# A transformer block on one core: the score products of a head pair moved from 122 shared rows to two 64-row halves of TensorE's array, with four slots and new instruction orders

## The chip, the cores and the metric

The kernel runs on one core of a Trainium2 chip. The metric is the device time of one execution in microseconds. Before the change the median of 3 runs is 1230.65 us (1229.91 to 1230.84).

## What is computed

The reference is one transformer block with adaptive layer norms for 32 sequences of 256 tokens and 288 channels, 16 heads of 18 channels, all in float32:

```python
B, L, C, H, D, FF = 32, 256, 288, 16, 18, 1152
ada = silu(c) @ W_ada + b_ada            # six vectors of 288 per sequence
shift_msa, scale_msa, gate_msa, shift_mlp, scale_mlp, gate_mlp = split(ada, 6)
h = layernorm(x) * (1 + scale_msa) + shift_msa
q, k, v = split_heads(h @ W_qkv + b_qkv)
attn = softmax((q * D ** -0.5) @ k.T)    # per head, 256 x 256
x = x + gate_msa * ((attn @ v) @ W_proj + b_proj)
h = layernorm(x) * (1 + scale_mlp) + shift_mlp
x = x + gate_mlp * (gelu(h @ W_fc1 + b_fc1) @ W_fc2 + b_fc2)
```

## The kernel before

The work goes sequence by sequence ("batch" b), and every engine runs a list of steps written out by hand: a head (`PE_HEAD` and so on), a period that is repeated for one batch after another (`PE_ORDER`), and a tail. An entry such as ("s", 1, 4) in a period for batch k is step `s` of batch k + 1 with number 4. `run` plays the lists. Between engines there are only semaphores, so a step that waits holds up all that stands behind it on its engine. Several batches are in flight: the scores of batch k, the projections of k + 2, the MLP of k - 2 and k - 3.

The matrix products take fp32r operands, split in a rounded part and a rest, so each projection is seven products (`products`): `xt` and `lt` turn the normalised tokens, `qk` and `v` project (bank `x_bank`), `proj`, `fc1`, `fc2` follow (banks `a_bank`, `b_bank`).

Attention works on pairs of heads: 8 pairs j per batch, in two halves of `HP` = 4. The q and k rows of a half are written to DRAM from `qst` (`qkw`) and read back (`qkr`, 13 DMAs per half) into slots of `ql` and `kl`. Three slots are used in turn (`half_use`). The rows of the contraction are a head's 54 rows (hi, lo and cross parts of 18 channels), at partitions 0 to 53 for head 0 and 68 to 121 for head 1, with four rows between at 64 to 67 (`MXR`). These four carry the row maxima: `kl` holds -1 in row 64 + j for pair j, `ql` the maximum of each query, so that the product gives scores minus maximum. `ql` has a block of its own for either head (index i), with zeros at the rows of the other head, and both heads share one `kl` block. One product contracts over all 122 rows.

- `s(b, j)` (L808) makes the scores of both heads, 2 products of 256 columns for each, into `score_bank[i]`. VectorE takes their maxima (`head_max`, L1138), transposes them (`mt`), and ScalarE copies them into the four rows of `ql` (`mb`, L946), 8 copies per half.
- `st(b, j)` (L822) makes the transposed scores less the maxima, 2 products of 512 columns (both heads at once), into `st_bank` of two PSUM banks; ScalarE takes `exp` into `e` (L953).
- `pv(b, half)` (L834) multiplies with v for the half: 16 fp32 products of 256 columns, each recorded as two, for four pairs in turn in four column tiles of 32.

In a slot that is used again, the four maxima rows must be zero before `s` runs; the 13th read of `qkr` (m == 12) does this by a DMA from a DRAM tensor `zeros` (L617). On SyncE's queue the reads of a half wait for the last `st` of the half that had the slot before.

```python
for i in range(2):
    wait(pe, s_max[i], PAIRS * b + j)
    for t in range(NT):
        last = nc.tensor.matmul(score_bank[i][:, t * L:(t + 1) * L],
                                ql[0:KM, slot, i, j % HP, t * P:(t + 1) * P], kl[0:KM, slot, j % HP, :],
                                start=True, stop=True)
    last.then_inc(s_full[i], 1)
```

Of the kernel before, what the change touches and what calls it, by code (L numbers as in the profile page):

```python
# [14 lines left out]
D = C // H  # L15
FF = 4 * C
EPS = 1e-6
P = 128
# [8 lines left out]
MXR = 64  # L27
HB = MXR + PAIRS // 2
KM = HB + KS
# [9 lines left out]
SLOTS = 3  # L39
# [4 lines left out]
READS = 13  # L44
# [32 lines left out]
    ("max", 0, 4), ("ln1_apply", 2, 0), ("max", 0, 5), ("om", -2, 1), ("qk", 1, 1), ("max", 0, 6), ("ol", -2, 1),  # L77
    ("max", 0, 7), ("fc1", -3, 4), ("rcp", -1, 0), ("mt", 0, 0), ("proj", -2, 0), ("proj", -2, 1), ("qk", 1, 2),
# [1262 lines left out]
```

## Time and profile before

| | |
|---|---|
| median of 3 runs | 1230.65 us |
| profiled execution | 1228.32 us |
| its span, first to last instruction | 1226.5 us |
| TensorE products busy | 1181.1 us, 96% |
| TensorE weight loads busy | 1064.3 us, 87% |
| VectorE busy | 901.8 us, 74% |
| ScalarE busy | 866.1 us, 71% |
| GpSimd busy | 540.3 us, 44% |
| mean granted TensorE clock | 0.993 |

How to read it. "PE" is TensorE's products, "PEld" its weight loads, DVE is VectorE, ACT ScalarE, POOL GpSimd, SP SyncE. A product's recorded duration includes its way through the array, so products overlap in the records; what one costs the queue is the distance from its start to the next start. Weight loads run ahead of products. A group row ends with the engine's idle time just before that group and what ended it.

### The profile page before, as it was taken

Reading aid. Unit: us, or ns where it says so; the run is one execution under the profiler, and the core shown is the slowest. Engines: PE = TensorE matmul, PEld = TensorE weight load, DVE = VectorE, ACT = ScalarE, POOL = GpSimd, SP = SyncE. Lnnn points to the kernel's source line nnn. Section 1 sums busy time; section 2 is a strip of 40 time slices with the busy share of each in tenths; the row PEclk is TensorE's granted clock in tenths of the full one; section 3 lists DMA queues with packets and bytes.
Section 4 is the critical chain, followed back from the end, with each engine's and each line's share of the span. In section 5 each row is a group of like instructions: output and inputs, shape, how many; then the busy total and the mean of one; then the engine's idle time right before and its main releaser. Section 6 shows DMA issues by size and latency. Waiting matters only on the chain.

```text
span 1226.5 us, 27564 instructions
## 1 busy us (share of the span) xinstructions
PE 1181.1 (96%) x9863; PEld 1064.3 (87%) x9863; DVE 901.8 (74%) x1928; ACT 866.1 (71%) x1485; POOL 540.3 (44%) x557
## 2 busy tenths in 40 slices
PE   6888999999999999999999999999999999999977
PEld 5666999999998999999999999999999999997777
DVE  5687777877777787778777777777777787775553
ACT  5387777777777777777777777777777777778721
POOL 3012544444454444445454444444444445443364
PEclk9799999999999999999999999999999999999999
DMA  8554555554555554445555444555554555444220
GB/s 265 171 169 138 167 167 164 164 154 144 163 160 159 168 166 145 157 157 162 167 166 164 147 159 150 166 165 167 161 153 148 158 166 159 162 149 140 87 68 20
DMA packets 134330, 188.91 MB, mean 154 GB/s; under 512 B 24544, under 2 KB 102422, under 8 KB 133947
## 3 DMA queue, kind: packets, MB, share of 16 engines
q1 hardware_dynamic: 134033, 186.71, 48.3%
q8 instruction: 80, 1.31, 0.5%
q10 hardware_dynamic: 162, 0.44, 0.1%
q14 instruction: 55, 0.45, 0.1%
HBM read 121.92 MB, written 64.63 MB: 152 GB/s over the span
## 4 chain that ended last, share of the span: by engine, by line
PE 84%; SPq 5%; DMA 4%; DVE 3%; ACT 2%; issue 1%; POOL 0%; ACTq 0%; POOLq 0%; DVEq 0%
PE a_bank L867 10%; PE x_bank L785 10%; PE score_bank L808 9%; PE turn_bank L834 9%; PE st_bank L822 9%; PE b_bank L867 8%; PE b_bank L881 6%; PE b_bank L882 5%; PE b_bank L883 5%; PE a_bank L848 4%; PE x_bank L793 4%; SPq L623 2%; DMA qk_rows<-qst 1%; DMA ql<-zeros 1%; PE x_bank L759 1%
## 5 line engine op out<-in xcount | busy, mean ns | idle before, releaser
L1138 DVE TENSOR_REDUCE mx<-score_bank 128x2 f32<-128x512 f32 x512 | 342.0, 687 | 95.8 <-PE score_bank L808 93.7
L953 ACT ACTIVATE e<-st_bank 128x1024 f32<-128x1024 f32 x256 | 262.4, 1025 | 125.8 <-PE st_bank L822 123.5
L1287 POOL TENSOR_TENSOR gl<-gl_raw,gh 128x512 fp32r<-128x512 f32 (+1 forms) x160 | 194.3, 1221 | 226.4 <-DVE gh L1203 226.4
L946 ACT CAST ql<-mxt 4x256 fp32r<-4x256 f32 x512 | 206.2, 403 | 7.4 <-DVE mxt L1147 0.6
L808 PEld LDWEIGHTS score_bank<-kl,ql 122*128 122x128 f32 x1024 | 146.9, 190 | 42.0 <-issue 24.4
L808 PE MATMUL score_bank<-kl,ql 122*128 122x256 f32 x1024 | 174.6, 293 | 5.6 <-DMA ql<-zeros 3.3
L881 PE MATMUL b_bank<-w,gh 128*128 128x288 f32 x576 | 174.5, 303 | 2.2 <-DVE tmp L1209 1.9
L822 PE MATMUL st_bank<-ql,kl 122*128 122x512 f32 x512 | 165.7, 405 | 7.7 <-ACT e L953 6.9
L882 PE MATMUL b_bank<-w,gh 128*128 128x288 f32 x576 | 170.5, 296 | 0.0
L883 PE MATMUL b_bank<-w,gl 128*128 128x288 f32 x576 | 170.3, 296 | 0.0
L834 PE MATMUL turn_bank<-e,ve 128*32 128x256 f32 x2048 | 123.8, 382 | 0.3 <-ACT e L953 0.3
L881 PEld LDWEIGHTS b_bank<-w,gh 128*128 128x128 f32 x576 | 108.8, 189 | 4.1 <-DVE tmp L1209 2.6
L867 PE MATMUL a_bank<-xh,w 128*128 128x256 f32 x640 | 105.4, 287 | 6.4 <-DVE xr L1117 4.4
L882 PEld LDWEIGHTS b_bank<-w,gh 128*128 128x128 f32 x576 | 108.9, 189 | 0.1
L883 PEld LDWEIGHTS b_bank<-w,gl 128*128 128x128 f32 x576 | 108.5, 188 | 0.0
L785 PE MATMUL x_bank<-xh,wq 128*128 128x256 f32 x632 | 103.1, 286 | 1.5 <-ACT xl_raw L920 0.8
L1203 DVE CAST gh<-gl_raw 128x512 fp32r<-128x512 f32 (+1 forms) x160 | 85.9, 551 | 18.6 <-ACT gl_raw L991 16.8
L834 PEld LDWEIGHTS turn_bank<-e,ve 128*32 128x32 f32 x2048 | 60.1, 110 | 43.0 <-issue 4.9
L1299 POOL TENSOR_TENSOR x<-tmp,x 128x288 f32<-128x288 f32 x64 | 51.8, 810 | 99.2 <-DVE tmp L1209 99.0
L867 PEld LDWEIGHTS a_bank<-xh,w 128*128 128x128 f32 x640 | 87.9, 191 | 8.7 <-issue 8.7
L822 PEld LDWEIGHTS st_bank<-ql,kl 122*128 122x128 f32 x512 | 79.8, 190 | 15.2 <-ACT e L953 10.4
L981 ACT ACTIVATE xl_raw<-a_bank,mod 128x256 f32<-128x256 f32 (+1 forms) x96 | 50.6, 561 | 59.8 <-PE a_bank L759 54.2
(152 smaller groups left out, 2473.1 us busy)
## 6 DMA issues: line engine op xcount, KB each, us to landing
qk_rows<-qst SPq DMA_DIRECT2D x128, 256.0 KB, 5.3
ql<-qk_rows SPq DMA_DIRECT2D x384, 72.0 KB
kl<-qk_rows SPq DMA_DIRECT2D x378, 72.0 KB
o_rows<-on SPq DMA_DIRECT2D x128, 128.0 KB
gate<-gates SPq DMA_DIRECT2D x32, 432.0 KB, 4.4
xin<-in_x SPq DMA_DIRECT2D x32, 288.0 KB, 5.9
x<-in_x SPq DMA_DIRECT2D x32, 288.0 KB, 3.0
out<-x SPq DMA_DIRECT2D x32, 288.0 KB, 4.5
```

Source lines behind the costliest of these rows:

```text
L785: last = nc.tensor.matmul(bank[:, k * L:(k + 1) * L], wa[:, c * P:(c + 1) * P], xa, start=(i == 0), stop=(i == len(pr) - 1))
L808: last = nc.tensor.matmul(score_bank[i][:, t * L:(t + 1) * L], ql[0:KM, slot, i, j % HP, t * P:(t + 1) * P], kl[0:KM, slot, j % HP, :], st ...
L822: last = nc.tensor.matmul(st_bank[:, u, :, :], kl[0:KM, slot, j % HP, u * P:(u + 1) * P], ql[0:KM, slot, :, j % HP, :], start=True, stop=True)
L834: last = nc.tensor.matmul(turn_bank[VB * c:VB * (c + 1), q * L:(q + 1) * L], ve[:, b % 2, u, 8 * half + 2 * c + q, :], e[:, c, u, q, :], s ...
L867: last = nc.tensor.matmul(bank[:, (f % 2) * L:(f % 2 + 1) * L], wa[:, f * P:(f + 1) * P], xa, start=(i == 0), stop=(i == len(pr) - 1))
L881: nc.tensor.matmul(b_bank[:, 0:C], gh[:, cols], w2[:, 0, f, :], start=(f == 0), stop=False)
L882: nc.tensor.matmul(b_bank[:, 0:C], gh[:, cols], w2[:, 1, f, :], start=False, stop=False)
L883: last = nc.tensor.matmul(b_bank[:, 0:C], gl[:, cols], w2[:, 0, f, :], start=False, stop=(f == NF - 1))
L946: last = nc.scalar.copy(rows[:, :, :, t, a, :], src)
L953: nc.scalar.activation(e[:, j % 4, :, :, :].rearrange("p u i l -> p (u i l)"), st_bank[:, :, :, :].rearrange("p u i l -> p (u i l)"), ACT. ...
L1138: nc.vector.tensor_reduce(mx[:, j // HP, i, :, col:col + 1], score_bank[i][:, :].rearrange("p (t l) -> p t l", t=NT), AX.X, ALU.max).then_ ...
L1287: nc.gpsimd.tensor_tensor(gl[:, cols], g[:, cols], gh[:, cols].bitcast(F32), ALU.subtract).then_inc(g_lo, 1)
```

## The change

The two heads of a pair get separate halves of the partitions. Head i has its rows from 64 i on: four rows for the maxima, then its 54 rows, 58 in all (`KM`). `ql` and `kl` lose the index for the head and the zero blocks, and each product contracts over the 58 rows of one head. In the built program these products have an array tile of 64 rows by 128 columns, at row 0 or 64, where they had the whole 128 by 128. `s` has 4 products of 256 columns as before, now issued t by t with the two heads in turn, after both waits. `st` has 4 products of 256 columns (two for each head, heads in turn) instead of 2 of 512, each head in its own bank of `st_bank`; `e` is laid out to match. The instruction that makes `exp` has the same size.

There are four slots instead of three. The four maxima rows are cleared by a GpSimd fill over rows 0 to 67 of the slot (`clear`, step "clr"), which waits for the last `st` of the half that had the slot, and `qkr` waits for the clear; the 13th read and the DRAM tensor `zeros` go, and there are 12 reads per half. The -1 rows of `kl` come from the identity matrix (`chosen`), by four ScalarE copies at the start, in place of fills, four DMAs and two ScalarE clears of `ql`.

The lists of all engines are new. Counted in the built programs, TensorE's queue changes its array tile 164 times before and 705 times after; in the repeated period it is 4 and 21 times. The period has 16 score steps (`s` or `st`); in the new list they stand in nine places, seven of two steps and two of one.

```diff
-MXR = 64
-HB = MXR + PAIRS // 2
-KM = HB + KS
+TILE = 64
+KM = PAIRS // 2 + KS
-SLOTS = 3
+SLOTS = 4
-READS = 13
+READS = 12
 PE_ORDER = [
-    ("fc2", -3, 2), ("pv", -1, 1), ("s", 0, 4), ("fc2", -3, 3), ("st", 0, 0), ("v", 1, 0), ("fc2", -3, 4),
...
+    ("fc2", -3, 0), ("proj", -2, 0), ("st", 0, 1), ("s", 0, 6), ("xt", 2, 0), ("proj", -2, 1), ("st", 0, 2),
...
-        ql = sb("ql", [P, SLOTS, 2, HP, L], F32R)
+        ql = sb("ql", [P, SLOTS, HP, L], F32R)
-        e = sb("e", [P, 4, NT, 2, L])
+        e = sb("e", [P, 4, 2, NT, L])
...
-            row = (0, HB)[i] + D * r
-            to = ql[row:row + D, slot, i, :, :] if w == 0 else kl[row:row + D, slot, :, :]
+            row = TILE * i + HP + D * r
+            to = (ql if w == 0 else kl)[row:row + D, slot, :, :]
...
-                    if use == 0:
-                        sp.wait_ge(consts, ROWS_SET)
-                        wait(sp, rows_cleared, slot)
-                    else:
-                        before = b * HALVES + half - SLOTS
-                        sp.wait_ge(st_full, PAIRS * (before // HALVES) + HP * (before % HALVES + 1))
-                if m == 12:
...
-                        sp.dma_start(ql[MXR:MXR + HP, slot, :, :, :].rearrange("p i j l -> p (i j l)").bitcast(F32),
-                                     zero_dram).then_inc(qk_rows[slot], 16)
-                    return
+                    if b == 0 and half == 0:
+                        sp.wait_ge(kl_chosen, SLOTS)
+                    sp.wait_ge(ql_cleared, HALVES * b + half + 1)
...
                 for i in range(2):
                     wait(pe, s_max[i], PAIRS * b + j)
-                    for t in range(NT):
+                for t in range(NT):
+                    for i in range(2):
+                        rows = slice(TILE * i, TILE * i + KM)
                         last = nc.tensor.matmul(score_bank[i][:, t * L:(t + 1) * L],
-                                                ql[0:KM, slot, i, j % HP, t * P:(t + 1) * P], kl[0:KM, slot, j % HP, :],
+                                                ql[rows, slot, j % HP, t * P:(t + 1) * P], kl[rows, slot, j % HP, :],
                                                 start=True, stop=True)
-                    last.then_inc(s_full[i], 1)
+                        if t == NT - 1:
+                            last.then_inc(s_full[i], 1)
...
                 for u in range(NT):
-                    last = nc.tensor.matmul(st_bank[:, u, :, :], kl[0:KM, slot, j % HP, u * P:(u + 1) * P],
-                                            ql[0:KM, slot, :, j % HP, :], start=True, stop=True)
+                    for i in range(2):
+                        rows = slice(TILE * i, TILE * i + KM)
+                        last = nc.tensor.matmul(st_bank[:, i, u, :], kl[rows, slot, j % HP, u * P:(u + 1) * P],
+                                                ql[rows, slot, j % HP, :], start=True, stop=True)
...
+            for u in range(SLOTS):
+                nc.gpsimd.memset(ql[0:TILE + HP, u, :, :].bitcast(F32), 0.0).then_inc(ql_cleared, 1)
+
+            def clear(b, half):
+                slot, use = half_use(b, half)
+                if use:
+                    before = b * HALVES + half - SLOTS
+                    pool.wait_ge(st_full, PAIRS * (before // HALVES) + HP * (before % HALVES + 1))
+                    nc.gpsimd.memset(ql[0:TILE + HP, slot, :, :].bitcast(F32), 0.0).then_inc(ql_cleared, 1)
```

How this moves TensorE's queue, first at the second `pv` of a period. Line numbers are those of either program; names are bank <- operands; `score_bank` is step `s`, `st_bank` step `st`, `turn_bank` step `pv`, `a_bank` and `b_bank` with `xh`, `xl`, `xr` are `fc1`, `x_bank` with `wq` is `qk`, `b_bank` with `gh`, `gl` is `fc2`. Before:

```order
L822 MATMUL st_bank<-ql,kl 128x512 x2
L808 MATMUL score_bank<-kl,ql 128x256 x4
L762 MATMUL x_bank<-ident,xn 96x128 x2
L867 MATMUL b_bank<-xh,w 128x256 x4
...
L834 MATMUL turn_bank<-e,ve 32x256 x16
L808 MATMUL score_bank<-kl,ql 128x256 x4
L867 MATMUL a_bank<-xh,w 128x256 x4
```

and after the change:

```order
L793 MATMUL score_bank<-kl,ql 128x256 x4
L822 MATMUL turn_bank<-e,ve 32x256 x16
L855 MATMUL a_bank<-xh,w 128x256 x4
L855 MATMUL a_bank<-xl,w 128x256 x2
L855 MATMUL a_bank<-xr,w 128x256
```

The score step stands in front of `pv` here and behind it before; the `st` step has 4 products of 256 columns in the new program. The next place is inside the period, between the MLP's products. Before:

```order
L785 MATMUL x_bank<-xr,wq 128x256
L808 MATMUL score_bank<-kl,ql 128x256 x4
L867 MATMUL b_bank<-xh,w 128x256 x4
L867 MATMUL b_bank<-xl,w 128x256 x2
L867 MATMUL b_bank<-xr,w 128x256
...
L867 MATMUL a_bank<-xr,w 128x256
L822 MATMUL st_bank<-ql,kl 128x512 x2
L808 MATMUL score_bank<-kl,ql 128x256 x4
```

and after:

```order
L871 MATMUL b_bank<-w,gl 128x288
L793 MATMUL score_bank<-kl,ql 128x256 x4
L810 MATMUL st_bank<-ql,kl 128x256 x4
L855 MATMUL a_bank<-xh,w 128x256 x4
...
L855 MATMUL a_bank<-xr,w 128x256
L793 MATMUL score_bank<-kl,ql 128x256 x4
L810 MATMUL st_bank<-ql,kl 128x256 x4
L768 MATMUL x_bank<-xh,wq 128x256 x4
```

A single score step and a pair of them stood here before; now the steps come in pairs with whole-array products between. Last, GpSimd's queue behind a `clr` in the new program:

```order
L1279 TENSOR_TENSOR x<-tmp,x 128x288
L1232 MEMSET ql 68x1024
L1285 TENSOR_TENSOR gl<-gl_raw,gh 128x256
L1279 TENSOR_TENSOR x<-tmp,x 128x288
L1262 TENSOR_TENSOR xl<-xl_raw,xh 128x512
```

The fill is new; what stood there before was the same subtraction (`fc1`) and residual additions (`proj`) without it.

## Rows read from the trace of the kernel before

**Rows 1.** The page's first part, and its chain of waits by engine

```profile
PE 1181.1 (96%) x9863; PEld 1064.3 (87%) x9863; DVE 901.8 (74%) x1928; ACT 866.1 (71%) x1485; POOL 540.3 (44%) x557
PE 84%; SPq 5%; DMA 4%; DVE 3%; ACT 2%; issue 1%; POOL 0%; ACTq 0%; POOLq 0%; DVEq 0%
```

**Rows 2.** Stretches: from:to and length, busy us (instructions) of each engine, clock, DMA

```profile
170.00:1050.00 880.00, 878.88 (x7504) 804.60 (x7506) 679.55 (x1458) 657.57 (x1132) 410.37 (x419) 1.00 0.50 159
600.50:636.13 35.63, 35.63 (x305) 32.66 (x304) 27.45 (x60) 26.69 (x46) 16.83 (x17) 1.00 0.54 168
0.00:100.00 100.00, 78.22 (x547) 60.42 (x547) 67.63 (x152) 58.11 (x97) 17.82 (x28) 0.93 0.65 196
```

**Rows 3.** Groups of instructions by line, 170 to 1050 us

```profile
L1138 DVE TENSOR_REDUCE mx<-score_bank 128x2 f32<-128x512 f32 x394 | 264.5, 687 | 70.4 <-PE score_bank L808 68.6
L953 ACT ACTIVATE e<-st_bank 128x1024 f32<-128x1024 f32 x199 | 204.0, 1025 | 104.3 <-PE st_bank L822 102.9
L946 ACT CAST ql<-mxt 4x256 fp32r<-4x256 f32 x392 | 157.9, 403 | 5.2
L1287 POOL TENSOR_TENSOR gl<-gl_raw,gh 128x512 fp32r<-128x512 f32 (+1 forms) x121 | 145.7, 1212 | 172.4 <-DVE gh L1203 172.4
L808 PE MATMUL score_bank<-kl,ql 122*128 122x256 f32 x784 | 131.8, 291 | 0.0
L822 PE MATMUL st_bank<-ql,kl 122*128 122x512 f32 x396 | 126.9, 402 | 1.1 <-ACT e L953 1.1
```

**Rows 4.** Timeline of TensorE's products: start us, us until the last ends

```profile
617.99 0.63 PE L822 MATMUL st_bank<-ql,kl 122*128 122x512 f32 x2
618.46 0.64 PE L808 MATMUL score_bank<-kl,ql 122*128 122x256 f32 x4
618.93 0.38 PE L762 MATMUL x_bank<-ident,xn 128*96 128x128 f32 x2
```

**Rows 5.** The same view around a `pv` step

```profile
604.74 0.29 PE L883 MATMUL b_bank<-w,gl 128*128 128x288 f32 x1
604.97 1.93 PE L834 MATMUL turn_bank<-e,ve 128*32 128x256 f32 x32
606.83 0.74 PE L808 MATMUL score_bank<-kl,ql 122*128 122x256 f32 x4
607.41 0.30 PE L881 MATMUL b_bank<-w,gh 128*128 128x288 f32 x1
```

**Rows 6.** The same view, products in flight at 606.49

```profile
606.28 0.40 PE L834 MATMUL turn_bank<-e,ve 128*32 128x256 f32 x4
```

**Rows 7.** Timeline of weight loads, those begun by 605.05 us

```profile
604.96 0.16 PEld L834 LDWEIGHTS turn_bank<-e,ve 128*32 128x32 f32 x8 [0.16 <-issue]
```

**Rows 8.** Timeline of weight loads around the same `pv` step

```profile
604.61 0.19 PEld L883 LDWEIGHTS b_bank<-w,gl 128*128 128x128 f32 x1
...
606.83 0.54 PEld L808 LDWEIGHTS score_bank<-kl,ql 122*128 122x128 f32 x4 [0.41 <-issue]
607.30 0.19 PEld L881 LDWEIGHTS b_bank<-w,gh 128*128 128x128 f32 x1
```

**Rows 9.** Timeline of weight loads of the modulation products

```profile
50.71 0.53 PEld L732 LDWEIGHTS st_bank<-rcb,e 128*128 128x128 f32 x4
51.28 0.30 PEld L732 LDWEIGHTS st_bank<-rcb,gh_raw 33*128 33x128 f32 x2
51.62 0.52 PEld L732 LDWEIGHTS st_bank<-rcb,e 128*128 128x128 f32 x4
```

**Rows 10.** Who waited for the DMAs that read `zeros`

```profile
  PEld score_bank L808: 5.4, 6
  PE score_bank L808: 3.3, 5
```

**Rows 11.** GpSimd's fills at the start, groups by line

```profile
L1233 POOL MEMSET kl<- 128x3072 f32 x1 | 2.7, 2657 | 3.8 <-DVE rcb L1033 3.8
L1234 POOL MEMSET ql<- 128x2048 f32 x1 | 1.8, 1822 | 0.0
```

More of the change, by code:

```diff
@@ new lines @@
+    ("max", 0, 11), ("ln1_stats", 3, 0), ("proj", -2, 0), ("fc1", -3, 4), ("max", 0, 12), ("max", 0, 13),
+    ("proj", -2, 1), ("rcp", -1, 1), ("max", 0, 14), ("max", 0, 15), ("xt", 2, 0), ("mt", 0, 1),
+    ("ln2_stats", -2, 0), ("xt", 2, 1), ("sum2", -3, 0), ("ln2_apply", -2, 0), ("ln2_apply", -2, 1), ("max", 1, 0),
+    ("max", 1, 1), ("qk", 2, 0), ("lt", -2, 0), ("max", 1, 2), ("max", 1, 3), ("lt", -2, 1), ("ln1_apply", 3, 0),
+    ("max", 1, 4), ("max", 1, 5), ("qk", 2, 1), ("sum2", -3, 1), ("max", 1, 6), ("max", 1, 7),
@@ L101 @@
+    ("or", -1, 0), ("qkr", 1, 12), ("qkr", 1, 13),
 ]
@@ L133 @@
+    ("v", 0, 0), ("qkr", 0, 0), ("v", 0, 1), ("qkr", 0, 1), ("qkr", 0, 2), ("qkr", 0, 3), ("qkr", 0, 4),
+    ("round", 0, 2), ("qkr", 0, 5), ("xt", 1, 0), ("xt", 1, 1), ("qk", 1, 0), ("round", 0, 3), ("round", 0, 4),
[9 rows of a table added]
 ]
 DVE_HEAD = [
[3 rows of a table removed]
-    ("max", 0, 2), ("max", 0, 3), ("ln1_apply", 2, 0), ("ln1_apply", 2, 1), ("max", 0, 4), ("max", 0, 5),
-    ("qk", 1, 1), ("max", 0, 6), ("max", 0, 7), ("mt", 0, 0), ("qk", 1, 2), ("max", 0, 8), ("max", 0, 9),
-    ("gates", 0, 0), ("mod", 0, 0), ("split", 0, 2), ("max", 0, 10), ("max", 0, 11), ("split", 0, 3), ("max", 0, 12),
@@ new lines @@
+    ("qkw", 3, 1), ("rr", 0, 1), ("qkw", 3, 2), ("rr", 0, 2), ("rr", 0, 3), ("or", 0, 4), ("rr", 0, 4), ("rr", 0, 5),
+    ("or", 0, 5), ("ow", 1, 0), ("qkr", 3, 0), ("qkw", 3, 3), ("sr", 1, 0), ("ow", 1, 1), ("qkr", 3, 1),
+    ("qkr", 3, 2), ("qkr", 3, 3), ("qkr", 3, 4), ("qkr", 3, 5), ("qkw", 3, 4), ("qkr", 3, 6), ("qkr", 3, 7),
+    ("qkr", 3, 8), ("qkr", 3, 9), ("qkr", 3, 10), ("sr", 1, 1), ("qkr", 3, 11), ("ow", 1, 2), ("ow", 1, 3),
+    ("sw", 1, 0), ("qkr", 3, 12), ("or", 1, 0), ("qkr", 3, 13),
@@ L224 @@
[L224 to L227 removed]
[10 rows of a table removed]
+    ("om", -4, 0), ("mt", -2, 0), ("max", -2, 8), ("fc1", -5, 0), ("fc1", -5, 1), ("qk", -1, 2), ("max", -2, 9),
@@ L270 @@
+    ("qkr", -1, 18), ("qkr", -1, 19), ("qkr", -1, 20), ("or", -3, 3), ("ow", -2, 0), ("rr", -3, 5), ("qkr", -1, 21),
[7 rows of a table added]
+    ("store", -2, 0), ("store", -1, 0),
 ]
@@ L698, in _ @@
                 load_weights(i)
-            sp.wait_ge(consts, ROWS_SET)
-            for jj in range(HP):
-                row = slice(MXR + jj, MXR + jj + 1)
-                sp.dma_start(kl[row, :, jj, :].bitcast(F32),
-                             tmp2[row, 0, 0:L].unsqueeze(1).broadcast_to([1, SLOTS, L])).then_inc(kl_rows, 16)
-            sp.dma_start(zero_dram, ql[MXR:MXR + HP, 0, :, :, :].rearrange("p i j l -> p (i j l)").bitcast(F32)
-                         ).then_inc(zeros_stored, 16)
             run(SYNC_HEAD, SYNC_ORDER, SYNC_TAIL, {"ln1_stats": ln1_stats, "res": res, "qkw": qkw, "qkr": qkr, "ow": ow,
@@ L903, in _ @@
             act.wait_ge(iota_step, 2)
-            for slot in range(1, SLOTS):
-                nc.scalar.activation(ql[:, slot, :, :, :].rearrange("p i j l -> p (i j l)"),
-                                     ident[:, 0:1].broadcast_to([P, 2 * HP * L]), ACT.Copy, scale=0.0
-                                     ).then_inc(rows_cleared, 1)
+            act.wait_ge(choice, 1)
+            for slot in range(SLOTS):
+                nc.scalar.activation(kl[0:TILE + HP, slot, :, :],
+                                     chosen[0:TILE + HP, :].unsqueeze(2).broadcast_to([TILE + HP, HP, L]), ACT.Copy,
+                                     scale=-1.0).then_inc(kl_chosen, 1)
             for i in range(N_FIRST):
@@ L941, in mb @@
                 act.wait_ge(mx_turned, HALVES * b + half + 1)
-                rows = ql[MXR:MXR + HP, slot, :, :, :].rearrange("p i j (t a x) -> p i j t a x", t=NT, x=VB)
-                for t in range(NT):
+                for i in range(2):
+                    rows = ql[TILE * i:TILE * i + HP, slot, :, :].rearrange("p j (t a x) -> p j t a x", t=NT, x=VB)
                     for a in range(P // VB):
-                        src = mxt[VB * a:VB * a + HP, half, :, t, :].unsqueeze(2).broadcast_to([HP, 2, HP, VB])
-                        last = nc.scalar.copy(rows[:, :, :, t, a, :], src)
+                        src = mxt[VB * a:VB * a + HP, half, i, :, :].unsqueeze(1).broadcast_to([HP, HP, NT, VB])
+                        last = nc.scalar.copy(rows[:, :, :, a, :], src)
                 last.then_inc(mx_rows, 1)
@@ L1336 @@
     args.append(nc.dram_tensor("r_rows", (2, HALVES, 4, 2, L), F32, kind="Internal").ap())
-    args.append(nc.dram_tensor("zeros", (HP, 2 * HP * L), F32, kind="Internal").ap())
     dit_block(nc, *args)
```

169 lines of the change are left out of this document (81 added, 88 removed), and 180 rows, old and new, of tables (ACT_HEAD, ACT_ORDER, ACT_TAIL, DVE_HEAD).

## Prediction

> **What bounds the kernel now.** I read the page's busy shares and its chain of waits first: TensorE is busy for 96% of the span, no other engine for more than 74%, and 84% of the chain that ends last is TensorE's own work [rows 1]. Then the table by stretches: from 170 to 1050 us TensorE is busy for 878.88 of 880.00 us, and a period of the repeated order (one batch) lasts 35.63 us and is full [rows 2]. So in the middle the time is what TensorE's queue takes, piece by piece, and nothing done on another engine shows unless it becomes late. VectorE waits there for score products, and ScalarE for transposed scores; they run behind TensorE with room [rows 3]. A term of the sum must therefore be read from distances between starts on TensorE, not from a product's duration, since products overlap.
>
> **What a score step costs now.** An `st` step (2 products of 512 columns) starts at 617.99, the `s` step behind it (4 products of 256 columns) at 618.46, and the next piece at 618.93 [rows 4]: 0.47 us each, or 0.118 us for 256 columns. There are 256 `s` and 256 `st` steps (1024/4 and 512/2 products over 32 batches), so 512 x 0.47 = 240.6 us of TensorE.
>
> **Part one, heads side by side.** Each product now uses 58 rows of a 64-row tile, at row 0 or 64, and the two heads of a pair are issued in turn into different PSUM banks. If two such products run together, a step is two rounds of 256 columns, 2 x 0.118 = 0.236 us, for `s` as for `st`. It saves 0.234 us per step, 512 x 0.234 = 119.8 us in all. That is the gross gain. What speaks for it in this trace is `pv`, whose four heads sit in four 32-column tiles: 32 products are recorded from 604.97 on, and the seventh round of four starts at 606.28, so a round of four takes (606.28 - 604.97)/6 = 0.218 us [rows 5, 6]; eight weight loads for it lie within 0.16 us [rows 7]. Tiles along the columns do run and load together. The bounds of a round along the rows are 0.11 us (four whole-array loads take 0.53 us of which the last lasts 0.19: (0.53 - 0.19)/3 [rows 8, 9]) and 0.235 us (one product after the other). I take 0.118, the distance that 256 columns show today.
>
> **Part two, the tile changes.** TensorE's array now changes between whole (128x128), half-row (64x128) and column (128x32) use. The built program changes tile 705 times, before 164 times: 541 more, 17 more in each period (21 against 4). What one costs stands in two places.
> - `pv` in the steady stretch. The last product before it starts at 604.74, `pv` at 604.97, the score step after it at 606.83 and the piece after that at 607.41 [rows 5]. A product of 288 columns takes 0.13, eight rounds 8 x 0.218 = 1.74, the score step 0.47. The stretch is 607.41 - 604.74 = 2.67, and 2.67 - 0.13 - 1.74 - 0.47 = 0.33 us is left for two changes. They are not alike. Going in, the weight loads are 0.35 us apart instead of 0.13 (604.61 to 604.96 [rows 7, 8]), 0.22 more, of which short 32-column loads give some back. Coming out, no weights are loaded until `pv` has drained: the first load and the first product both stand at 606.83 [rows 5, 8], and what follows is 0.11 us later again.
> - The modulation products at 50.7 us go to 33 rows (a 64x128 tile) and back. Four weight loads start at 50.71, the next two in the half-row tile at 51.28, the next four, whole again, at 51.62 [rows 9]. At 0.11 us per load the four and the two would take 0.44 and 0.22 us; they take 0.57 and 0.34. Each change costs 0.12 us, **in both directions, and it is this very pair of tiles**. But these products have only 32 columns.
>
> Both places fit one picture: at a change the next load waits until the last product has streamed through and drained. Behind a product of 32 columns, which by the rounds of `pv` streams for 0.218 x 32/256 = 0.03 us, that adds 0.12 us; a product of 256 columns streams for 0.118 us, 0.09 longer, which gives 0.21. The load gap at `pv` says 0.22, of which a short load gives some back. I take 0.20 us, since products of 256 and 288 columns stand on both sides of nearly every change. The ends are 0.12 and 0.22. So 541 x 0.20 = 108 us is paid, with ends 65 and 119.
>
> **Part three, the new order** puts an `st` and an `s` next to each other in seven of nine visits of a period; two visits have a single step. Two steps cost 4 x 0.118 + 2 x 0.20 = 0.87 against 0.94 before: 0.07 gained. A single one costs 0.236 + 0.40 = 0.64 against 0.47: 0.17 lost. A period gains 16 x 0.234 = 3.74 and pays 17 x 0.20 = 3.40: **0.34 us net of 35.63**. Over 880/35.63 = 24.7 periods that is 8.4 us. The head and the tail hold the rest of the steps (118 of 512: 784/4 + 396/2 = 394 lie in the middle [rows 3]) and 541 - 17 x 24.7 = 121 changes; 118 x 0.234 - 121 x 0.20 = 3.4 us, of which I count half, because TensorE waits there anyway (78.22 busy of the first 100 us [rows 2]).
>
> **Part four, the fills.** 61 DMAs that clear four rows from `zeros` go; TensorE's products waited 3.3 us for them and its loads 5.4 us in the same waits [rows 10]. I take 3 us off; the ends are 0 (the `q` and `k` rows land as late) and 5. In their place GpSimd clears 68 rows of 1024 values, 60 times in the loop and 4 times at the start. Fills of 3072 and 2048 values take 2.66 and 1.82 us [rows 11], 0.82 per 1024, so one takes about 0.98 us and all 59 us more on an engine busy 44% [rows 1]. Nothing on TensorE waits for GpSimd but `g_lo`, whose engine itself waits 172.4 us for VectorE in the middle [rows 3]: cost nothing, and if that cover were gone at most the 59 us. Each clear waits for the `st` steps of four halves ago, and the `qkr` reads on SyncE's queue wait for the clear; behind it stand `ln1`, the MLP's subtractions and `sum2`. The fourth slot gives this chain a half-batch more than before, so I charge nothing. The `mb` copies stay 8 per half of 4x256 values (403 ns [rows 3]), `exp` and the maxima keep their shapes. The kept constants of `kl` are written by four ScalarE copies where two larger ones cleared `ql`: same size in all.
>
> **Sum.** -8.4 - 1.7 - 3 = -13 us. The profiled execution took 1228.32 us for its span of 1226.5, and lies 2.3 us under the median of 1230.65, so the median becomes about **1218 us**, 1% faster. It is a small difference of two large numbers: 0.012 us more per round, or 0.024 us more per change, takes all of it away.
>
> **The rivals.**
> 1. *Half-row weight loads do not overlap* (slower). Each step needs four loads of 128 columns at 0.11 us, before only four for `s` and two for `st`. If loads for the lower and the upper half go one after the other, a step lasts 4 x 0.11 = 0.44, saves 15 us in all, and still pays 108: 1230.65 + 93 - 3 = **1321 us**. For it: the trace has no half-row tiles loading next to each other, and loads are busy 804.60 of 880 us already [rows 2]. Against it: column tiles load together. It decides from a round of 0.13 us on, where 1024 rounds no longer pay for the changes. The Trainium skill (TensorE: Matmul & The Clock Gate, Part 3) says a weight load overlaps products in flight only when the row group differs; by that rule the second round of each half would wait for the first, and the time would come out like this rival's. The trace disagrees with it in whole-array use, where the four loads of a score step, 0.54 us with the last one's 0.19, run while its products do, 0.12 us apart [rows 5, 8]. The same page gives 3.07x for four row tiles, which speaks against this rival; no row here shows it. Chance 0.20.
> 2. *Cheap changes* (faster). If a change costs 0.12 us as in the modulation products, 541 x 0.12 = 65, net gain 119.8 - 65 + 3 = 58: some **1173 us**; 0.16 gives 1195. For it: it is the only place with this pair of tiles. Against it: the products there are short. Chance 0.13.
> 3. *The tight new order is late* (slower). A score bank and the `st` bank are single: `s` now waits for both heads' maxima before its first product, and each change adds a place where TensorE cannot run ahead. If two of a period's 16 steps wait 0.5 us each, 24.7 us come on top of the forecast: **1243 us**. For it: `s` and `st` now come in bunches, with `exp` at 1.03 us each. Against it: VectorE and ScalarE are idle a quarter of a period [rows 2]. Chance 0.17.
>
> **How the numbers follow.** The forecast case, rounds of 0.11 to 0.125 us and changes of 0.18 to 0.22, has 0.50 and runs from 1203 to 1233. A measurement of this kernel tells 0.2%, 2.5 us, from no change. Within that band lies the top of the forecast case and the bottom of rival 3, 0.08. Faster: 0.13 from rival 2 and 0.45 from the forecast, 0.58. Slower: 0.20 + 0.14, 0.34. The range leaves out rival 1 alone and takes in the whole of rival 2 and rival 3 with some room: 1172 to 1260. The forecast's own range is 1203 to 1233.
>
> **What would show it.** Right: `s` and `st` groups about 0.24 us between starts inside a visit, pairs of products with starts a few ns apart, weight loads some 0.3 us apart across each change, a period near 35.3 us, TensorE without waits. Rounds of 0.2 us, a period over 38 us, would be rival 1; changes of 0.12 and a period near 34 us rival 2; waits of TensorE for VectorE's maxima, ScalarE's `exp` or the reads behind GpSimd's clears rival 3. The prediction is wrong if the period falls outside 34.6 to 36.5 us.

## The result, and the profile after

The changed kernel takes **1203.48 us** (median of 4 runs, 1201.41 to 1204.61), the kernel before 1230.74 us beside it (4 runs, 1229.91 to 1231.61). The ratio on record is 0.976, with a 95% interval of 0.9737 to 0.9784 (the quotient of these two medians alone is 0.978, inside it): 2.4% faster, where 1% was forecast (1218 us). The profiled execution took 1203.89 us for a span of 1202.1 us, 24.4 us less span than before.

First the page's busy shares and its chain of waits by engine:

```profile
PE 1158.4 (96%) x10375; PEld 993.9 (83%) x10375; DVE 920.6 (77%) x1928; ACT 858.0 (71%) x1485; POOL 579.2 (48%) x619
PE 92%; DVE 3%; ACT 2%; DMA 1%; issue 1%; SPq 0%; POOL 0%; ACTq 0%; POOLq 0%; DVEq 0%
```

TensorE bounds the kernel as before and is busy for 22.7 us less [rows 1]; the shares of SyncE's queue and the DMAs in the chain shrink from 9% to 1%. Then the stretches of the same kind as [rows 2]; the second is one period of the repeated order:

```profile
0.00:100.00 100.00, 77.59 (x547) 58.47 (x548) 61.96 (x143) 52.44 (x90) 18.33 (x32) 0.83 0.65 193
600.47:635.32 34.85, 34.85 (x321) 30.23 (x320) 28.15 (x59) 26.48 (x47) 17.96 (x19) 1.00 0.51 158
170.00:1030.00 860.00, 860.00 (x7904) 745.48 (x7904) 694.73 (x1458) 655.57 (x1142) 446.92 (x473) 1.00 0.52 162
```

A period lasts 34.85 us instead of 35.63, and TensorE is busy for all 860 us of the middle. The first 100 us differ in one more thing: the granted clock is 0.83 there and was 0.93. Most of that is one stretch, in the changed kernel's trace first and in that of before second:

```profile
55.50:73.00 17.50, 16.92 (x95) 11.13 (x94) 12.71 (x25) 12.71 (x25) 2.96 (x4) 0.51 0.55 168
55.50:73.00 17.50, 15.62 (x117) 12.03 (x116) 15.98 (x34) 13.32 (x23) 2.13 (x3) 1.00 0.48 147
```

TensorE ran there at the lower of its two levels, 1.2 GHz, after 10.5 us in which it had been busy for 8.1; before the change it was busy for all of the same 10.5 us and kept 2.4 GHz, and so it did in c_whole, the run with the new orders and no half-row tile, busy for 8.6 us there. The prediction has no term for this, and no run isolates what it costs. The groups that answer to [rows 3], and GpSimd's new fill, from 170 to 1030 us:

```profile
L1128 DVE TENSOR_REDUCE mx<-score_bank 128x2 f32<-128x512 f32 x392 | 254.1, 685 | 66.2 <-PE score_bank L793 65.5
L942 ACT ACTIVATE e<-st_bank 128x1024 f32<-128x1024 f32 x196 | 200.8, 1024 | 132.5 <-PE st_bank L810 132.3
L935 ACT CAST ql<-mxt 4x256 fp32r<-4x256 f32 x400 | 160.7, 402 | 4.1
L1285 POOL TENSOR_TENSOR gl<-gl_raw,gh 128x512 fp32r<-128x512 f32 x100 | 135.6, 1366 | 145.1 <-DVE gh L1193 145.1
L1232 POOL MEMSET ql<- 68x1024 f32 x50 | 47.5, 950 | 0.0
```

The maxima, `exp` and the `mb` copies keep their durations to 1 or 2 ns. A fill takes 0.95 us (the estimate was 0.98), and GpSimd still waits 145 us for VectorE before `g_lo`.

Now the score products. The timeline at the visit that the period begins with (start us, us until the last ends, count):

```profile
600.24 0.30 PE L836 MATMUL a_bank<-wp,orem 119*128 119x288 f32 x1
600.47 0.30 PEld L810 LDWEIGHTS st_bank<-ql,kl 58*128 58x128 f32 x4 [0.17 <-issue]
600.47 0.50 PE L810 MATMUL st_bank<-ql,kl 58*128 58x256 f32 x4
600.69 0.31 PEld L793 LDWEIGHTS score_bank<-kl,ql 58*128 58x128 f32 x4
600.81 0.40 PE L793 MATMUL score_bank<-kl,ql 58*128 58x256 f32 x4
601.14 0.44 PE L742 MATMUL x_bank<-ident,xn 128*128 128x128 f32 x2
```

Four half-row loads lie within 0.30 us, where four whole-array ones need 0.54 [rows 8]. In the single records the two halves' loads start 3 to 5 ns apart, and so do their products. From the start of one pair of products to the start of the next it is 0.117 and 0.118 us here, and 0.118 on average in the steady part, wherever no change lies between. So a round of two half-row products of 256 columns lasts 0.118 us, as long as one whole-array product did [rows 4]. From 600.47 to 601.14 two steps take 0.67 us, against 0.94 in [rows 4]; the price of entering shows in front of them (0.23 us from the 288-column product at 600.24, which streams for 0.13) and inside the first step (0.22 us between its two rounds).

Where the 24.4 us of span went, by the distances between the first `pv` steps of successive batches:

| stretch | before | after | difference |
|---|---|---|---|
| start to the fourth such `pv` | 156.3 | 153.6 | -2.7 |
| the 25 periods behind it | 892.2 | 871.3 | -20.9 |
| the rest | 178.0 | 177.2 | -0.8 |

Of the -20.9, 25 x 0.78 = 19.5 is the shorter period; 1.3 us is a single wait of TensorE for `exp` in one period of the trace before (1.1 us at 386 us) that the trace after does not have.

### The profile page after: what moved, and what is told of

Same layout as the page of the kernel before. It is cut to its first block, busy times and chain, and to the rows that moved or that the text cites. A ratio compares the mean times of both kernels' runs of the same rounds, so it can differ in the third digit from the quotient of the medians.

```text
span 1202.1 us, 28774 instructions
## 1 busy us (share of the span) xinstructions
PE 1158.4 (96%) x10375; PEld 993.9 (83%) x10375; DVE 920.6 (77%) x1928; ACT 858.0 (71%) x1485; POOL 579.2 (48%) x619
## 4 chain that ended last, share of the span: by engine, by line
PE 92%; DVE 3%; ACT 2%; DMA 1%; issue 1%; SPq 0%; POOL 0%; ACTq 0%; POOLq 0%; DVEq 0%
PE a_bank L855 13%; PE x_bank L768 12%; PE turn_bank L822 10%; PE b_bank L855 9%; PE score_bank L793 7%; PE st_bank L810 7%; PE b_bank L869 7%; PE b_bank L870 6%; PE b_bank L871 6%; PE a_bank L836 5%; PE x_bank L776 5%; PE x_bank L742 2%; PE a_bank L742 1%; ACT e L942 1%; PE x_bank L745 1%
## 5 line engine op out<-in xcount | busy, mean ns | idle before, releaser
L1128 DVE TENSOR_REDUCE mx<-score_bank 128x2 f32<-128x512 f32 x512 | 332.3, 685 | 94.6 <-PE score_bank L793 92.8
L869 PE MATMUL b_bank<-w,gh 128*128 128x288 f32 x576 | 179.1, 311 | 2.0 <-DVE tmp L1199 1.9
L870 PE MATMUL b_bank<-w,gh 128*128 128x288 f32 x576 | 170.6, 296 | 0.0
L871 PE MATMUL b_bank<-w,gl 128*128 128x288 f32 x576 | 169.6, 295 | 0.0
L810 PE MATMUL st_bank<-ql,kl 58*128 58x256 f32 x1024 | 117.9, 309 | 6.1 <-ACT e L942 5.0
L793 PE MATMUL score_bank<-kl,ql 58*128 58x256 f32 x1024 | 120.7, 314 | 2.7 <-DVE mx L1128 1.9
L855 PE MATMUL a_bank<-xh,w 128*128 128x256 f32 x640 | 112.2, 298 | 5.5 <-DVE xr L1107 4.0
L768 PE MATMUL x_bank<-xh,wq 128*128 128x256 f32 x632 | 111.9, 300 | 2.2 <-DVE qst L1120 1.3
L1193 DVE CAST gh<-gl_raw 128x512 fp32r<-128x512 f32 (+1 forms) x160 | 92.7, 594 | 23.0 <-ACT gl_raw L980 22.0
L870 PEld LDWEIGHTS b_bank<-w,gh 128*128 128x128 f32 x576 | 108.7, 189 | 0.0
L871 PEld LDWEIGHTS b_bank<-w,gl 128*128 128x128 f32 x576 | 108.6, 189 | 0.0
L855 PEld LDWEIGHTS a_bank<-xh,w 128*128 128x128 f32 x640 | 87.4, 191 | 25.4 <-issue 15.1
L768 PEld LDWEIGHTS x_bank<-xh,wq 128*128 128x128 f32 x632 | 87.6, 193 | 20.2 <-issue 16.0
L793 PEld LDWEIGHTS score_bank<-kl,ql 58*128 58x128 f32 x1024 | 78.4, 188 | 30.9 <-issue 19.9
L810 PEld LDWEIGHTS st_bank<-ql,kl 58*128 58x128 f32 x1024 | 78.0, 187 | 29.8 <-issue 15.5
```

The costliest lines, as they stand in the source:

```text
L768: last = nc.tensor.matmul(bank[:, k * L:(k + 1) * L], wa[:, c * P:(c + 1) * P], xa, start=(i == 0), stop=(i == len(pr) - 1))
L810: last = nc.tensor.matmul(st_bank[:, i, u, :], kl[rows, slot, j % HP, u * P:(u + 1) * P], ql[rows, slot, j % HP, :], start=True, stop=True)
L855: last = nc.tensor.matmul(bank[:, (f % 2) * L:(f % 2 + 1) * L], wa[:, f * P:(f + 1) * P], xa, start=(i == 0), stop=(i == len(pr) - 1))
L869: nc.tensor.matmul(b_bank[:, 0:C], gh[:, cols], w2[:, 0, f, :], start=(f == 0), stop=False)
L870: nc.tensor.matmul(b_bank[:, 0:C], gh[:, cols], w2[:, 1, f, :], start=False, stop=False)
L871: last = nc.tensor.matmul(b_bank[:, 0:C], gl[:, cols], w2[:, 0, f, :], start=False, stop=(f == NF - 1))
```

## The experiments

Nine kernels ran, all of them edits of the changed kernel; "period" is the distance between first `pv` steps in the steady stretch. The ratios go by the kernel before as it ran beside each: 1234.12 us for a_turn, b_split, c_whole and j_shalf, 1236.28 for k_onehalf, e_clear2, f_best1 and g_both, 1235.11 for h_pv0. So ratios and periods can be compared between rows, medians only roughly.

| run | median us | ratio to before (95%) | period us |
|---|---|---|---|
| changed kernel | 1203.48 | 0.976 (0.9737 to 0.9784) | 34.85 |
| a_turn | 1209.34 | 0.9796 (0.9761 to 0.983) | 34.92 |
| b_split | 1283.77 | 1.0406 (1.0375 to 1.0437) | 37.71 |
| c_whole | 1228.66 | 0.9961 (0.9943 to 0.9979) | 35.67 |
| j_shalf | 1253.94 | 1.0166 (1.0125 to 1.0206) | 36.53 |
| k_onehalf | 1329.03 | 1.0769 (1.0717 to 1.082) | 38.70 |
| e_clear2 | 1208.17 | 0.9778 (0.9746 to 0.9809) | 34.85 |
| f_best1 | 1322.97 | 1.071 (1.0673 to 1.0748) | 38.2 to 41.2 |
| g_both | 1343.35 | 1.0877 (1.0837 to 1.0918) | 38.6 to 40.8 |
| h_pv0 | 1213.49 | 0.9825 (0.9797 to 0.9853) | 35.11 |

**c_whole: the new orders, slots and clears without half-row tiles.** The steps contract over all 122 rows again.

```diff
-                        rows = slice(TILE * i, TILE * i + KM)
+                        rows = slice(0, TILE + KM)
...
-                                     scale=-1.0).then_inc(kl_chosen, 1)
+                                     scale=-0.5).then_inc(kl_chosen, 1)
```

> The changed kernel in everything (orders, four slots, GpSimd clears, 12 reads, four products per step) but that each score product contracts over all 122 rows of the whole array, so both heads' scores are summed and the constant rows hold -0.5; the scores are not those of the reference. It is the new order without half-row tiles. If tiles and their changes make the whole difference: 16 steps of 0.47 us and 4 changes as before, period 35.5 to 35.7 us, and 1222 to 1230 us (the head and tail keep what the new order gained there). Rival, that the new order also packs TensorE better: period below 35.2 us and a time under 1215 us.

It takes 1228.66 us, 0.4% less than before (ratio 0.9943 to 0.9979, 3 to 7 us), with a period of 35.67 us. So everything of the change but the tiles gives little, and the two traces do not show where: the start, up to the fourth `pv`, takes 154.1 us, near the changed kernel's 153.6, instead of 156.3; the 25 periods behind it take 891.9 instead of 892.2; the rest takes 180.4 instead of 178.0. The step from here to the changed kernel, 0.9961 to 0.976, is the tiles: 0.82 us per period.

Both kernels issue the same pieces in the same order, so the two traces can be laid over each other. Timeline of c_whole, at the three kinds of visit (a pair of steps before transposes, a pair before `fc1`, a single step):

```profile
611.12 0.30 PE L836 MATMUL a_bank<-wp,orem 119*128 119x288 f32 x1
611.26 0.65 PE L810 MATMUL st_bank<-ql,kl 122*128 122x256 f32 x4
611.74 0.65 PE L793 MATMUL score_bank<-kl,ql 122*128 122x256 f32 x4
612.23 0.60 PE L742 MATMUL x_bank<-ident,xn 128*128 128x128 f32 x4
612.59 0.77 PE L836 MATMUL a_bank<-wp,oh 126*128 126x288 f32 x4
...
615.83 0.29 PE L871 MATMUL b_bank<-w,gl 128*128 128x288 f32 x1
615.96 0.64 PE L810 MATMUL st_bank<-ql,kl 122*128 122x256 f32 x4
616.44 0.30 PE L869 MATMUL b_bank<-w,gh 128*128 128x288 f32 x1
616.58 0.29 PE L870 MATMUL b_bank<-w,gh 128*128 128x288 f32 x1
...
629.03 0.29 PE L871 MATMUL b_bank<-w,gl 128*128 128x288 f32 x1
629.16 0.64 PE L793 MATMUL score_bank<-kl,ql 122*128 122x256 f32 x4
629.63 0.64 PE L810 MATMUL st_bank<-ql,kl 122*128 122x256 f32 x4
630.12 0.65 PE L855 MATMUL a_bank<-xh,w 128*128 128x256 f32 x4
630.60 0.41 PE L855 MATMUL a_bank<-xl,w 128*128 128x256 f32 x2
```

and the changed kernel's at the end of the first kind (its beginning stands above), and at the two others:

```profile
601.55 0.38 PE L836 MATMUL a_bank<-wp,oh 126*128 126x288 f32 x1
...
604.63 0.30 PE L871 MATMUL b_bank<-w,gl 128*128 128x288 f32 x1
604.86 0.51 PE L810 MATMUL st_bank<-ql,kl 58*128 58x256 f32 x4
605.30 0.40 PE L869 MATMUL b_bank<-w,gh 128*128 128x288 f32 x1
605.53 0.30 PE L870 MATMUL b_bank<-w,gh 128*128 128x288 f32 x1
...
617.70 0.29 PE L871 MATMUL b_bank<-w,gl 128*128 128x288 f32 x1
617.92 0.50 PE L793 MATMUL score_bank<-kl,ql 58*128 58x256 f32 x4
618.26 0.40 PE L810 MATMUL st_bank<-ql,kl 58*128 58x256 f32 x4
618.59 0.74 PE L855 MATMUL a_bank<-xh,w 128*128 128x256 f32 x4
619.17 0.40 PE L855 MATMUL a_bank<-xl,w 128*128 128x256 f32 x2
```

A whole-array step lasts 0.478 us on average here (the one in front of `pv`, 0.57, left out), two rounds 0.236, so half-row tiles save 0.242 us per step, and what is missing of that is the price of two changes:

| visit | whole | half-row | difference | one change |
|---|---|---|---|---|
| pair, then transposes (L836 to L836) | 1.47 | 1.31 | -0.16 | (0.484 - 0.16)/2 = 0.16 |
| pair, then `fc1` (L871 to second L855) | 1.57 | 1.47 | -0.10 | (0.484 - 0.10)/2 = 0.19 |
| single in `fc2` (L871 to L870) | 0.75 | 0.90 | +0.15 | (0.242 + 0.15)/2 = 0.20 |

Over one whole period, piece by piece, the four visits before transposes gain 0.14 to 0.16 each, the three other pairs 0.10 to 0.11, the single before `pv` gains 0.05 and the single in `fc2` loses 0.15: 0.81 us in all. On average a change costs (16 x 0.242 - 0.82)/17 = **0.18 us**: 0.17 in the four visits before transposes (their mean gain is 0.147), 0.19 elsewhere.

**b_split: more changes.** The seven pairs of the period are pulled apart, no work added. In the list that was built `st` 6 of one batch and `s` 3 of the next come to stand side by side anew, so a period has 33 changes, 12 more and not the 14 of the expectation. The edit as one of its seven places:

```diff
-    ("fc2", -3, 0), ("proj", -2, 0), ("st", 0, 1), ("s", 0, 6), ("xt", 2, 0), ("proj", -2, 1), ("st", 0, 2),
+    ("fc2", -3, 0), ("proj", -2, 0), ("st", 0, 1), ("xt", 2, 0), ("s", 0, 6), ("proj", -2, 1),
```

> The changed kernel with its seven pairs of neighbouring score steps pulled apart in TensorE's repeated list (one piece of other work put between the two steps of each pair): 14 more tile changes per period, the same products. At 0.18 us per change, which the changed kernel's period of 34.85 us suggests, the period becomes 37.4 us and the time about 1270 us; at the 0.20 us of the prediction 37.65 us and 1277 us; at the 0.12 us of the modulation products 36.5 us and 1247 us. Rival, that a change is hidden by waits in any case: period under 35.5 us.

The period grows by 2.86 us. The one wait of TensorE from 500 to 900 us (total, times, longest):

```profile
PE a_bank L746 <- ACT xl_raw L971: 5.5, 11, 0.5
```

That is 0.5 us once per period, since the layer norm's second transposes now come too early for ScalarE. Between starts it costs 0.57: the `s` step in front of these transposes takes 1.01 us to the next start, the others that stand alone 0.43. The remaining 2.29 us over 12 changes is 0.19 us each. Where transposes are what stands between the two steps, two more changes cost 0.36 to 0.39 us against the changed kernel's pair, 0.18 to 0.195 each, so the lower price seen before transposes does not hold in every order; what makes it was not tested.

**j_shalf: half-row tiles for `s` alone.** `st` contracts over 122 rows, so nearly every pair has a change in its middle.

```diff
@@ step st
-                        rows = slice(TILE * i, TILE * i + KM)
+                        rows = slice(0, TILE + KM)
```

> The changed kernel, but only s uses half-row tiles; st contracts over all 122 rows of the whole array (summed heads, not the reference's values). 8 steps save 0.24 us each against whole-array use, and s alone needs 15 tile changes more than the kernel before. At 0.18 us per change: 35.63 - 1.92 + 2.70 = 36.4 us per period, about 1247 us; at 0.20 us 36.7 us, 1255 us; at 0.12 us 35.5 us, 1225 us. It checks the price of a change and the saving of a round by another mix of the two than the pulled-apart order.

The period is 36.53 us, 0.86 more than with no half-row tile at all: half of the gain (8 x 0.242 = 1.94 us) pays for 15 of the 17 changes, (1.94 + 0.86)/15 = 0.19 us each. This side of the trade is the one that the prediction's small difference warned of.

**k_onehalf: both heads on the same half.** The products have the same shape and number; the upper half of the array is never used.

```diff
@@ steps s and st
-                        rows = slice(TILE * i, TILE * i + KM)
+                        rows = slice(0, KM)
```

> The changed kernel, but all four products of every step read the rows of head 0, so all run on the lower half of the array (the second head's values are left out). The tile changes are the same. The pulled-in-turn order made no difference, so this asks what the second half is worth: if the halves work side by side, putting all on one gives four rounds instead of two, +0.115 x 32 = 3.7 us per period, a period of 38.5 us and about 1315 us. Rival, that a product of 58 rows is simply cheaper in either half: period stays 34.85 us, 1203 us.

The period grows by 3.85 us, 32 rounds x 0.120. The visit in its timeline, behind a `fc2` product:

```profile
601.66 0.30 PE L871 MATMUL b_bank<-w,gl 128*128 128x288 f32 x1
601.89 0.53 PEld L793 LDWEIGHTS score_bank<-kl,ql 58*128 58x128 f32 x4 [0.17 <-issue]
601.89 0.74 PE L793 MATMUL score_bank<-kl,ql 58*128 58x256 f32 x4
602.47 0.64 PE L810 MATMUL st_bank<-ql,kl 58*128 58x256 f32 x4
603.04 0.42 PE L745 MATMUL a_bank<-ident,xn 128*96 128x128 f32 x2
```

Four loads of the same half take 0.53 us instead of 0.30, and two steps 1.15 instead of 0.67. The whole gain is two halves at work at once, not the fewer rows of a product. With them one after the other the change would have cost 7.7%.

**a_turn: the heads one after the other.** The two products of head 0 are issued before those of head 1, in `s` and in `st`.

```diff
-                for t in range(NT):
-                    for i in range(2):
+                for i in range(2):
+                    for t in range(NT):
```

> The changed kernel, but the products of a step are issued head by head (both of head 0, then both of head 1) instead of in turn. If the gain comes from the two halves of the array loading and multiplying at the same time, then only the second product of head 0 and the first of head 1 can still overlap: three rounds of 0.115 us per step instead of two, +0.115 x 16 = 1.8 us per period, a period of 36.7 us and a time near 1260 us. Rival, that the halves are free of the issue order: period stays 34.85 us, 1203 us. Rival, that head by head nothing overlaps: four rounds, period 38.5 us, some 1320 us.

The period is 34.92 us, 0.07 more than in turn, and the ratios' intervals overlap. The timeline:

```profile
601.92 0.30 PEld L810 LDWEIGHTS st_bank<-ql,kl 58*128 58x128 f32 x4 [0.45 <-ACT e L942]
601.93 0.51 PE L810 MATMUL st_bank<-ql,kl 58*128 58x256 f32 x4 [0.22 <-ACT e L942]
602.27 0.40 PE L793 MATMUL score_bank<-kl,ql 58*128 58x256 f32 x4
```

Four loads still lie within 0.30 us and the products still start in pairs, 4 to 12 ns apart, although two products of the same half follow each other in the program. In the single records of all 256 `s` steps the product that raises the signal of head 0, its second, stands in the later pair. So head 1's first product starts before head 0's second, which the program has in front of it. The theory that the turn-taking makes the overlap fell; "heads issued in turn" is not where the gain is.

**e_clear2: twice the clearing.** A second fill of the same size into a spare tile follows each clear on GpSimd.

```diff
+                    wait(pool, spare_set, b * HALVES + half - SLOTS)
+                    nc.gpsimd.memset(spare[0:TILE + HP, :], 0.0).then_inc(spare_set, 1)
```

> The changed kernel with a second fill of the same size into a spare tile behind each of GpSimd's clears: 60 more fills of 0.95 us. The prediction priced the clears at nothing, because TensorE waits for nothing on GpSimd that is late: period 34.85 us, within 0.2% of the changed kernel. Rival, that GpSimd's queue is near the edge: each fill on the path adds up to 0.95 us, period up to 36.7 us, 1260 us.

The period stays at 34.85 us in nearly all periods; the start up to the fourth `pv` grows by 3.3 us (first `pv` at 69.6 instead of 68.1, third distance 35.8 instead of 34.6), and the ratio's interval overlaps the changed kernel's. The first added fill stands at 71.4 us, so 1.5 of the 3.3 us came before any of them. In the steady part the clears cost nothing.

**Three versions meant to be faster.** Each of f_best1, g_both and h_pv0 saves one to three changes per period by moving steps in TensorE's list, with no work added or left out; in g_both and h_pv0 ScalarE's list changes too, so that it copies the first `pv` after the first part of `qk`. f_best1 issues each of the next batch's scores one visit earlier (20 changes), g_both also puts both `pv` steps in front of score steps (18 changes):

```diff
@@ f_best1
-    ("s", 0, 7), ("xt", 2, 1), ("fc2", -3, 1), ("st", 0, 3), ("fc2", -3, 2), ("pv", 0, 0), ("qk", 2, 0),
-    ("fc2", -3, 3), ("s", 1, 0), ("st", 0, 4), ("lt", -2, 0), ("fc2", -3, 4), ("s", 1, 1), ("st", 0, 5),
+    ("st", 0, 2), ("s", 0, 7), ("xt", 2, 1), ("fc2", -3, 1), ("st", 0, 3), ("s", 1, 0),
+    ("fc2", -3, 2), ("pv", 0, 0), ("qk", 2, 0), ("fc2", -3, 3), ("st", 0, 4), ("s", 1, 1),
@@ g_both
+    ("fc2", -3, 2), ("qk", 2, 0), ("fc2", -3, 3), ("pv", 0, 0), ("st", 0, 4), ("s", 1, 1),
...
+    ("qk", 2, 2), ("fc1", -2, 1), ("fc1", -2, 2), ("v", 2, 0), ("fc1", -2, 3), ("pv", 0, 1),
```

> The changed kernel with s(1, j) of TensorE's repeated list one visit earlier, so that the 16 steps stand in eight pairs; 20 tile changes per period instead of 21. At 0.18 us per change: period 34.67 us, -4.7 us in all, about 1199 us. Rival, that the earlier scores wait for VectorE's maxima or for the q and k rows: period 35 us or more.

> As the run with eight pairs, and both pv steps moved to stand directly in front of a pair of score steps (ScalarE copies the first pv after the qk part instead of before it): 18 tile changes per period instead of 21. At 0.18 us per change: period 34.31 us, -14 us in all, about 1189 us. Rival, that the later pv makes the exp behind it late or that a change between column and half-row tiles costs more: period 34.7 us or more.

Both lose 7 to 9%. TensorE's waits from 500 to 900 us, of f_best1:

```profile
PE score_bank L794 <- DVE mx L1129: 16.5, 16, 1.6
PE score_bank L794 <- DMA kl<-qk_rows: 13.4, 10, 1.7
```

and of g_both:

```profile
PE score_bank L795 <- DVE mx L1130: 16.7, 16, 1.6
PE score_bank L795 <- DMA kl<-qk_rows: 16.1, 10, 2.0
```

The scores of the next batch have no room to move up: their k rows have not landed and the bank's maxima have not been taken. These waits are 30 and 33 us in 400, while f_best1's periods of 39.2 us on average lose 44 us in the same stretch. TensorE is busy for 370 and 365 of the 400 us, and its granted clock is 0.98 and 0.97 there instead of 1.00; how the rest of the loss divides was not separated. h_pv0 moves only the first `pv` a few products later, right in front of the pair (20 changes):

```diff
-    ("s", 0, 7), ("xt", 2, 1), ("fc2", -3, 1), ("st", 0, 3), ("fc2", -3, 2), ("pv", 0, 0), ("qk", 2, 0),
-    ("fc2", -3, 3), ("s", 1, 0), ("st", 0, 4), ("lt", -2, 0), ("fc2", -3, 4), ("s", 1, 1), ("st", 0, 5),
+    ("st", 0, 2), ("s", 0, 7), ("xt", 2, 1), ("fc2", -3, 1), ("st", 0, 3), ("fc2", -3, 2),
+    ("qk", 2, 0), ("fc2", -3, 3), ("pv", 0, 0), ("s", 1, 0), ("st", 0, 4), ("lt", -2, 0),
```

> The changed kernel with the first attention-times-values step of a pair moved right in front of the two score steps of the next visit, so that the whole-array product before these scores is one that had to run anyway and one change between whole-array and half-row products falls away per period (20 instead of 21); no work is added or left out. Theory (a change of tile costs about 0.18 us, and nothing waits for this step): the period goes from 34.85 to 34.67 us, over some 26 periods about 5 us less, a time near 1199 us. Rival 1 (the later product makes the copy of the pair's output late, and the maxima or the exponentials shift into a wait of TensorE): period at or above 34.85 us, 1204 us or more, and a wait of TensorE for ScalarE or VectorE stands in the steady part. Rival 2 (the moved product's own end costs more than the products it stood among): period 34.8 to 34.9, no difference that can be measured.

Of the first rival the period and a wait of TensorE for VectorE came, but not its cause, a late copy of `pv`. The wait from 170 to 1020 us:

```profile
PE x_bank L770 <- DVE xr L1109: 4.6, 23, 0.2
```

`qk` now stands where `pv` had covered VectorE's subtraction for it, and waits 0.2 us in each period. Between starts this costs more than the idle time:

```profile
612.36 0.39 PE L770 MATMUL x_bank<-xl,wq 128*128 128x256 f32 x2
612.96 0.39 PE L770 MATMUL x_bank<-xr,wq 98*128 98x256 f32 x1 [0.20 <-DVE xr L1109]
613.18 0.64 PE L770 MATMUL x_bank<-xh,wq 128*128 128x256 f32 x4
```

The two `xl` products take 0.60 us where they take 0.24 in the changed kernel, the `xr` product 0.22 where it takes 0.12: 0.46 us in all. The saved change gives back 0.09 in front of `qk` and 0.10 in its first products. That leaves 0.27, and the period is 0.26 longer, 35.11 us. The third distance between `pv` steps is 38.9 us instead of 34.6; its cause is open. No version here beats the changed kernel.

The old layout with the new orders was not tried; c_whole stands in for it.

## Why the prediction was right in direction and short by half

The forecast was 13 us under the profiled execution of 1228.32 us, that is 1215.3; the profiled execution of the changed kernel took 1203.89, 11.4 us less. The other 3 us of the distance from 1218 to 1203.48 are the 2.3 us by which the profiled execution of before lay under its median, and the changed kernel's did not, and rounding. The measured 1203.48 lies inside the range, in the case forecast as likeliest, at its edge (1203 to 1233). The period, 34.85 us, is inside the limits set for it (34.6 to 36.5), but 0.44 us under the forecast's 35.3.

**Part one, the saving of a step.** Mechanism and size right: two rounds per step for `s` and `st` alike, and a round of 0.118 us as taken. A whole-array step was taken as 0.47 from one place [rows 4]; in the form and order of the new program it would last 0.478 (c_whole), so against c_whole the saving is 0.242 us per step and not 0.234, 0.13 us per period.

**Part two, the price of a change.** **This is the step that failed**: 0.20 us was set for every change "since products of 256 and 288 columns stand on both sides of nearly every change", and a change costs 0.18 on average, 17 x 0.18 = 3.06 us per period and not 3.40. Where such products stand on both sides it is 0.19 to 0.20, and the single step of 0.64 us comes out to the hundredth (0.90 - 2 x 0.13). But in four of nine visits transposes stand behind, which is in the new list and was not priced. There a pair of changes costs 0.34 instead of 0.40, 0.25 us per period for the four; the other 0.09 is 0.01 less on each of the other nine. The trade of 3.74 gained against 3.40 paid was a small difference of large terms, as the prediction said: 3% more of the one and 10% less of the other more than doubled it, to 0.82 (c_whole to the changed kernel). In sum: -0.34 - 0.13 - 0.34 = -0.81 for the tiles, where 0.82 was measured. Against the kernel before 0.78 is left, since c_whole's period is 0.04 us longer than that kernel's. The middle also gained the wait of 1.3 us that stands in one period of the trace before; the forecast has nothing for it, and one trace cannot tell it from chance.

**Part three, head and tail.** Start and rest together give 3.5 us where 1.7 plus 3 for the fills was forecast. By the traces of one execution each it is put together otherwise: without half-row tiles (c_whole) the start is 2.2 us shorter than before and the rest 2.4 longer, so orders, slots and fills give nothing in all, and the 3 us for the DMAs from `zeros` do not show. The tiles give 0.5 at the start and 3.2 in the rest, near the full 3.4 of which the prediction counted half. That the sum came near 4.7 is luck in part, and the lower clock of the start stands against it at a price that was not measured.

**Part four, the fills.** Right for the steady part: GpSimd's 0.95 us clears are hidden, and so is a second one behind each. TensorE's wait for the `zeros` DMAs [rows 10] is gone from the trace, but no time is seen to come of it (part three).

**The rivals.** Rival 1 (loads of the two halves do not overlap) did not come; k_onehalf, with every product on one half, comes close to what it would have been: 1329 us against the 1321 worked out for it. The rule of the Trainium skill (TensorE: Matmul & The Clock Gate, Part 3) that a load overlaps products in flight only when the row group differs is contradicted a second time: in k_onehalf all four loads of a step go to the same half and lie within 0.53 us, under the products of that half, as in whole-array use. The same section also lets a load into a background weight buffer run ahead, and with that these traces agree. Rival 2 (changes of 0.12 us) did not come either; before transposes the price, 0.17, goes a third of the way. Rival 3 (the tight order waits) did not come for this order: TensorE is busy for all of 860 us. f_best1 and g_both show that it lies one visit away.

## What to carry to other kernels

When a change trades many small savings against many small costs, read each price at every kind of neighbour that the new order has, not at the commonest: the sum hangs on the differences. Products whose contraction fits 64 rows can run two at a time on TensorE's two halves and then cost half, but each group of them pays a little under 0.2 us to enter and again to leave, so a step that saves 0.24 us pays only in groups of two or more, or where it stands against a change that is paid anyway (the single step before `pv` gained 0.05). An order in which nothing waits can still have no room: look at what stands ready behind each step before moving it up to save a change.

## What the runs showed of the hardware that was not expected

- Two products for different halves start together in both orders of issue that ran: 4 to 12 ns apart in the visit shown with the same half issued twice in a row (a_turn), 3 to 5 ns in turn. In a_turn a product for one half starts ahead of an earlier one for the other half.
- Leaving a half-row group costs less before transposes: laid over c_whole, the pieces behind lose 0.04 to 0.055 us there and 0.09 to 0.10 us before ordinary products. The price is paid in four places: 0.09 us in front of the group, 0.10 in its second round (0.22 instead of 0.118 us after the first), 0.09 behind its last round (0.21 instead of 0.12, 600.93 to 601.14), and the rest at the second product behind it (605.30 to 605.53 above, 0.23 instead of 0.14).
- Four loads of 58 rows take 0.53 us when their half is alone (k_onehalf), and four of 122 rows take 0.54 [rows 8], so fewer rows alone save nothing.
- A wait can cost more than the idle time that the profile lists for it: 0.2 us of waiting put 0.46 us between starts in h_pv0, 0.5 us put 0.57 in b_split.
